# Cross attention and experts on one core: where the rough pairs stand in TensorE's order

## The reference

```
def xattn(x, context):                      # 16 heads of 64
    q, k, v = x @ Wq, context @ Wk, context @ Wv
    scores = einsum('bqhd,bkhd->bhqk', q, k) * scale
    attn = softmax(scores)
    return einsum('bhqk,bkhd->bqhd', attn, v) @ Wo + bo

x = x + xattn(layernorm(x), ctx)
x = x + ffn(layernorm(x))    # 8 experts, each takes the 513 rows with the highest router score;
                             # gelu(tokens @ w1 + b1) @ w2 + b2, gated, scattered back by addition
```

## Time and profile before

| | us |
|---|---|
| median of 3 runs | 1501.13 |
| lowest and highest | 1500.43, 1507.04 |
| the profiled execution | 1498.66 |
| its span, first to last instruction | 1496.9 |
| TensorE busy | 1358.9 |
| VectorE busy | 965.3 |
| GpSimd busy | 970.3 |
| ScalarE busy | 695.5 |

### The profile page before, as it was taken

One profiled execution on the slowest core, in us unless ns is written; L12 is line 12 of the kernel. 1 busy time (PEld: TensorE's weight loads), 2 busy tenths in 40 slices (PEclk: granted clock), 3 DMA queues, 4 the chain that ended last, 5 costly groups with the idle time before them and its releaser, 6 DMA issues. The chain is left out here.

```text
span 1496.9 us, 24049 instructions
## 1 busy us (share of the span) xinstructions
PE 1358.9 (91%) x8354; PEld 854.1 (57%) x8354; DVE 965.3 (64%) x1632; ACT 695.5 (46%) x883; POOL 970.3 (65%) x497
## 2 busy tenths in 40 slices
PE   4989999999999999999999999999968814999995
PEld 3745555555555555555455555554438704998995
DVE  7666767776776777677677677777426564665552
ACT  2325544554554555455455455554533112755652
POOL 3217987887797787788679878878865003345443
PEclk8989999999999999999999999999979855999998
DMA  8440001001001000100100010010126232344422
GB/s 240 152 147 1 23 16 59 16 16 59 16 23 40 29 16 22 52 22 16 54 15 23 20 55 15 16 50 20 67 85 223 71 114 88 90 127 120 97 34 25
DMA packets 75471, 88.76 MB, mean 59 GB/s; under 512 B 10427, under 2 KB 55516, under 8 KB 75356
## 3 DMA queue, kind: packets, MB, share of 16 engines
q1 hardware_dynamic: 68572, 78.32, 15.8%
q0 software_dynamic: 6784, 8.94, 3.7%
HBM read 58.98 MB, written 27.99 MB: 58 GB/s over the span
## 5 line engine op out<-in xcount | busy, mean ns | idle before, releaser
L93 DVE TENSOR_REDUCE mx_part<-ps_m 128x1 f32<-128x512 f32 x744 | 478.6, 685 | 280.0 <-PE ps_m L81 273.5
L770 POOL TENSOR_TENSOR acc_p<-acc_p,x_in 128x1024 f32<-128x1024 f32 x224 | 558.1, 2491 | 151.9 <-ACT x_in L851 146.4
L851 ACT ACTIVATE x_in<-ps_s 128x1024 f32<-128x1024 f32 x384 | 380.2, 1022 | 254.5 <-PE ps_s L675 149.5
L698 PE MATMUL ps_o<-x_in,v 128*64 128x512 f32 x1664 | 406.2, 606 | 0.0
L675 PE MATMUL ps_s<-q,k 64*128 64x512 f32 x2496 | 386.1, 396 | 0.0
L675 PEld LDWEIGHTS ps_s<-q,k 64*128 64x128 f32 x2496 | 268.7, 185 | 47.9 <-ACT x_in L851 5.7
L81 PE MATMUL ps_m<-k,q 64*128 64x512 f32 x744 | 246.8, 479 | 8.0 <-DVE mx_part L93 3.5
L81 PEld LDWEIGHTS ps_m<-k,q 64*128 64x128 f32 x744 | 99.8, 185 | 176.5 <-issue 100.7
L698 PEld LDWEIGHTS ps_o<-x_in,v 128*64 128x64 f32 x1664 | 99.5, 136 | 163.1 <-issue 135.6
L1402 POOL DMA_INDIRECT xg<-table,idx_g x40 | 46.0, 1151 | 139.0 <-DVE idx_g L1392 129.2
L770 DVE TENSOR_TENSOR acc_d<-acc_d,x_in 128x1024 f32<-128x1024 f32 x64 | 118.0, 1843 | 15.4 <-ACT x_in L851 13.6
(11 more groups left out here) (256 smaller groups left out, 1946.7 us busy)
## 6 DMA issues: line engine op xcount, KB each, us to landing
w_in<-in_w SPq DMA_DIRECT2D x16, 1024.0 KB, 5.0
v_st<-rec_scr SPq DMA_DIRECT2D x64, 128.0 KB, 2.9
o_scr<-v_st SPq DMA_DIRECT2D x32, 256.0 KB, 2.1
v_scr<-c_in SPq DMA_DIRECT2D x13, 512.0 KB, 2.6
v<-v_scr SPq DMA_DIRECT2D x8, 832.0 KB, 5.5
ot<-o_scr SPq DMA_DIRECT2D x2, 2048.0 KB, 11.2
x_in<-in_x SPq DMA_DIRECT2D x4, 512.0 KB, 7.4
x<-in_x SPq DMA_DIRECT2D x4, 512.0 KB, 10.8
```

What stands on the lines that cost most here:

```text
L93: dve.tensor_reduce(part[:, j // S.MF, j % S.MF:j % S.MF + 1], bank[:, 0:S.MC], AX.X, ALU.max).then_inc(G.rough_used[hd], 1)
L698: last = pe.matmul(ps_o[hd * HP:hd * HP + DH, :], v[b][:, s, hd * DH:(hd + 1) * DH], probs[:, g % RING, hd * QC:(hd + 1) * QC], start=(s = ...
L770: eng.tensor_tensor(acc, other, probs[:, (u * KT + t) % RING, :], ALU.add).then_inc(done, 1)
L851: act.activation(probs[:, g % RING, :], ps_s[:, g % 2, :], ACT.Exp, bias=G.pad_bias[:, 0:1] if s == KT - 1 else 0.0, scale=SCALE).then_inc ...
```

## The change

TensorE's order in a group. Scores of the first slot now come ahead of its rough pair. In a double group the scores of the second slot follow, then the first of the products with the values, then the second slot's rough pair, no longer split, then the second product. Group 0 has scores, rough pair, two products; group (1, 2) has scores, rough, scores, product, rough. No instruction is added or taken away, and the other engines' lists are as before.

```diff
-            def scores(u, s, then_rough=False):
+            def scores(u, s):
...
                 for n in range(3):
-                    if n == 2 and then_rough:
-                        rough(u, s, (0,))
-                        pe_score(pe, g, u, s, b, n, 1)
-                        pe_score(pe, g, u, s, b, n, 0)
-                        rough(u, s, (1,))
-                    else:
-                        for hd in range(2):
-                            pe_score(pe, g, u, s, b, n, hd)
+                    for hd in range(2):
+                        pe_score(pe, g, u, s, b, n, hd)
...
                 for n, group in enumerate(GROUPS):
+                    other, products = u if n else u - 1, GROUPS[n - 1]
+                    scores(u, group[0])
                     rough(u, group[0])
-                    for s in group:
-                        scores(u, s, then_rough=(s != group[0]))
-                    for s in GROUPS[n - 1]:
-                        values(u if n else u - 1, s)
+                    for s in group[1:]:
+                        scores(u, s)
+                    values(other, products[0])
+                    for s in group[1:]:
+                        rough(u, s)
+                    for s in products[1:]:
+                        values(other, s)
                     small(u, group[-1])
```

## The result

| | before | changed |
|---|---|---|
| median, us | 1502.59 (4 runs) | 1523.91 (4 runs) |
| lowest and highest | 1500.43, 1507.04 | 1523.62, 1524.26 |
| span of the profiled execution | 1496.9 | 1522.4 |

The ratio is 1.0138, 95% interval 1.0113 to 1.0163: slower by 21 us. Forecast were 1521.5 and +21.5 over the profiled execution. A later set of runs gave 1.0142 (1.0119 to 1.0165).

A forecast was written before the change was run, and what follows sets the result against it. TensorE's own instruction row was taken as the bound, counted by matmul starts. The order's 22.7 us less 1 was summed as +21.5; over the profiled 1498.66 us, plus 2.5 for the median, 1521.5 was forecast, range 1508 to 1531.

The forecast's parts named there:

- The price of a change of kind: On TensorE, switching between 64-row and full-array steps: each way in or out costs about 0.1 us over the pitch.
- first row pair 0.33: On TensorE, the first 64-row pair behind a values product lasts 0.33 us instead of 0.23.
- V block of one slot 1.01: One slot's product with the values takes 1.01 us to whatever is next; a two-slot block takes 1.87.
- lone R 0.43: A rough pair (one matmul per head) alone between two full-array steps costs 0.43 us instead of 0.23.
- Rival A: Change of kind is hidden and only the double groups' 0.24 stall goes: 30 us faster, 1471; chance 6%.
- The stall of 0.24 in a double group: The split second rough pair's head 1 waits for VectorE's reduces, 0.15 + 0.09 us; the change removes it.
- Slots 1 and 2: Group of slots 1 and 2 with one product: 3.31 us before, 3.49 after, +0.18 a unit.
- The correction of -1 us: Slots 1 and 2's 0.43 stall in half the units stays, less 0.05 x 15; if it vanished, 6.5 us.
- rival C: More waits on VectorE, adds pushing reduces past their rough pair; one more a unit is 13 us: 1535; chance 7%.
- The order's 22.7: TensorE's new order adds 0.74 us a unit: 31 x 0.74 - 0.22 = 22.7 us.

The follow-up runs named there:

- the cut without a lone R: Kernel before, with the first product placed between the two slots' scores in two-product double groups, second rough pair still split: 1512.58 us, ratio 1.0153.
- half reduces: VectorE's rough-bank reduce over 256 of 512 columns: on the kernel before 1440.86 us, ratio 0.9696; on the changed kernel 1496.66 us, ratio 1.0068.
- Written out: Loop over pairs of heads written out: kernel before 1495.26 us, ratio 0.9981; changed kernel 1511.01, 1.0088; kernel before with VectorE's add moved 1490.49, 0.9955.
- moved add: Kernel before, with VectorE's add of tile 12 ahead of slot 0's two reduces instead of behind them: 1483.76 us, ratio 0.9961.
- uncut products: Changed kernel, with the two products together again behind the second rough pair: 1624.12 us (one run), 126 over the kernel before.

## Why the prediction was right, point by point

- **What bounds.** Right. In the attention TensorE's starts set the end, with VectorE's waits seen in them; reading starts, not drawn lengths, gave each piece to 0.02 us.
- **The price of a change of kind** (first row pair 0.33, V block of one slot 1.01, lone R 0.43). Right, and shown: 4.26 in the profile after, and the cut without a lone R cost the same (4.29). Rival A fell with it. The Trainium skill's rule in "TensorEngine Tiling (Array Packing)", Tiling Modes, Key Properties, that a change of tiling mode drains the engine, agrees with what these two orders show; no run here varies the mode alone. So that the changes of kind cost this much is shown, and why they do is not.
- **The stall of 0.24 in a double group.** Right in mechanism and size (3.92 with half reduces). The group of slots 7 and 8 hid 0.15 more that I had not seen; it did not enter the sum, which took that group's 4.30 as measured. The waits that remain are 22, where some 15 were forecast.
- **Slots 1 and 2.** The regular part is right: a unit without a stall on either side grew 0.69 to 0.72, 0.74 forecast.
- **The correction of -1 us** is the step that failed. I let the stall of slots 1 and 2 stand since I took the add behind slot 0 to last 2.56 in the same units. In the profile after it is 1.22 in all units but the last ones, and the stall is gone: -0.43 x 15 = -6.5 us, the very figure given as the other end. That VectorE comes to it at another moment of the unit is my reading of why it is short. The long duration went to the add behind slot 8 (3.22 at 702.45), which makes reduces 9 and 10 late in one unit of four: +0.55 x 8 = +4.4 us. That is rival C's mechanism in a place I did not name.
- **The jumps.** Not in the sum at all, and not in any rival. Two gaps between passes of the loop and the clock behind them added 4.3 us in the profile. Nor was the end of the attention: the last three units grew by 4.5 us, with a wait for VectorE and a third fall of the clock. Written out, the orders are 15.8 us apart.
- **The adding up.** 22.7 less 1 is 21.7 and not 21.5, which changes nothing.

So the number is right partly by luck. The order's 22.7 is right. Two misses on VectorE, -6.5 and +4.4, nearly cancel and leave 20.6; the regular units' 0.61 makes 19 over 31 units, and the jumps and the last units, which were in no term, bring the rest.

## What to carry to other kernels

Where TensorE alternates between 64-row pairs and full-row steps and is never idle, count the changes of kind before anything is moved: here each way out and back cost 0.35 us, more than the 0.24 us stall it removed, and a wait view that fell from 141 to 22 said nothing of it. A stall that another engine causes can be cheaper to cure on that engine: moving one VectorE add took 5.6 us off, where reordering TensorE added 21 (it cured the 0.43 of slots 1 and 2, not the 0.24). Before a step is moved, measure the distance that its bank needs (here 1.8 us from one rough pair to the next) against all neighbours, the group ahead included; the two times I did not, it cost 11 us and 7 us.

## What the runs showed that I had not expected

- An elementwise add of the same shape on VectorE took from 1.22 to 3.45 us, depending on where it fell in the unit. I suspect GpSimd's adds running at the same time. In seven of the profiles, 672 adds, the 112 that lay beside none of GpSimd's elementwise instructions took 1.21 to 1.23 us, every one over 1.4 lay beside one, and no add spent more than 1.23 us outside them. But 32 lay beside one in full and took no more than 1.25. So the long ones go with GpSimd's work, which alone does not decide, and no run here takes that work away.
- At a loop's jump the start of the last block of products and the next start on TensorE were 2.4 to 3.9 us apart in eleven profiles, with no rule by the block ahead or the instruction behind. The clock fell to 1.2 GHz for 3.4 us behind some: behind both jumps in each of two profiles of the changed kernel, behind neither in that of before, and behind one of two in five variants, where the gaps were 2.83 to 3.87. Gaps of 3.84 (moved add) and 3.93 (uncut products) had no fall. What decides it stays open.
